# Convolutions and mixings on array tiles of 32 rows and 64 columns instead of 32 rows and 128 columns

## The reference

```python
# x: (128, 128, 2048)  batch, channel, length;   cond: (128, 128);   fside: (128,)
def conv_layer(x, c, weight, c_weight, bias):        # weight (128, 32, 9), 4 groups
    out = lax.conv_general_dilated(x, weight, window_strides=(1,), padding=[(4, 4)],
                                   dimension_numbers=('NCH', 'OIH', 'NCH'), feature_group_count=4)
    return out + jnp.einsum('nd,od->no', c, c_weight)[:, :, None] + bias[None, :, None]

def mixing_layer(x, emb, W0, b0, W1, b1, W2, b2, weight, bias_k):   # weight (8, 128, 128, 1)
    h = gelu(gelu(emb @ W0 + b0) @ W1 + b1)
    att = softmax(h @ W2 + b2)                         # one weighting of 8 experts per sample
    agg_w = jnp.einsum('bk,koi->boi', att, weight[..., 0])
    return jnp.einsum('boi,bih->boh', agg_w, x) + (att @ bias_k)[:, :, None]

x = x + conv_layer(x, cond, w0, c_w0, fside);   x = x + mixing_layer(x, cond, ...)   # layers 0, 1
x = x + conv_layer(x, cond, w2, c_w2, fside);   x = x + mixing_layer(x, cond, ...)   # layers 2, 3
```

## Time and profile before

| | |
|---|---|
| median of 3 runs | 2659.2 us (2658.6 to 2659.79) |
| profiled execution | 2658.37 us, span 2656.6 us |
| PE busy | 2588.4 us (97%), 24,812 matmul records |
| weight loads (PEld) | 1191.4 us (45%) |
| DVE busy | 2148.2 us (81%) |
| ACT busy | 1493.2 us (56%) |
| POOL busy | 36.7 us (1%) |
| DMA | 357.06 MB, mean 134 GB/s |

### The profile page before, as it was taken

The page is one execution under the profiler, slowest core; times in us unless marked ns, Lnnn a source line. Parts: engine busy times, 40 slices in busy tenths (PEclk is TensorE's granted clock), DMA queues, the critical chain, the costliest instruction groups (busy, mean ns, idle before and its releaser), DMA issues.

```text
span 2656.6 us, 57542 instructions
## 1 busy us (share of the span) xinstructions
PE 2588.4 (97%) x24812; PEld 1191.4 (45%) x24812; DVE 2148.2 (81%) x815; ACT 1493.2 (56%) x852; POOL 36.7 (1%) x31
## 2 busy tenths in 40 slices
PE   6689999999999999999999999999999999999998
PEld 4234444444444444444444444444444444444443
DVE  5678888888888888888888888888888888888883
ACT  2345555555555555555555555555555555555554
POOL 5000000000000000000000000000000000000000
PEclk8689999999999999999999999999999999999999
DMA  4543444434434434444344344343443443443433
GB/s 151 205 163 118 155 121 130 146 118 136 140 118 146 130 119 152 123 127 149 118 139 137 118 150 126 120 154 120 132 144 118 139 137 118 148 128 120 153 92 112
DMA packets 185493, 357.06 MB, mean 134 GB/s; under 512 B 12714, under 2 KB 143794, under 8 KB 152634
## 3 DMA queue, kind: packets, MB, share of 16 engines
q1 hardware_dynamic: 184576, 352.37, 42.3%
q10 hardware_dynamic: 898, 4.39, 0.7%
HBM read 205.72 MB, written 150.99 MB: 134 GB/s over the span
## 4 chain that ended last, share of the span: by engine, by line
PE 96%; DMA 2%; DVE 1%; ACT 1%; issue 0%; ACTq 0%; SPq 0%; DVEq 0%
PE psum L350 34%; PE psum L313 33%; PE psum L325 28%; DMA mix_dram<-y 1%; DVE diff L545 0%; DVE y L594 0%; ACT y L464 0%; DMA select_sb<-select 0%; PE psum L274 0%; ACT y L474 0%; PE psum L303 0%; DMA mixw<-mix_dram 0%; ACT x L514 0%; ACT outb L498 0%; DVE att L565 0%
## 5 line engine op out<-in xcount | busy, mean ns | idle before, releaser
L545 DVE TENSOR_TENSOR diff<-xin 128x2052 f32<-128x2052 f32 x256 | 986.7, 3897 | 354.9 <-PE psum L325 354.9
L350 PE MATMUL psum<-y,mixw 32*128 32x512 f32 x8192 | 917.8, 595 | 20.1 <-DMA mixw<-mix_dram 13.7
L313 PE MATMUL psum<-diff,prod_w 32*128 32x512 f32 x8192 | 907.8, 589 | 12.5 <-DVE bias_table L584 7.6
L325 PE MATMUL psum<-diff,prod_w 32*128 32x512 f32 (+1 forms) x8192 | 773.2, 600 | 0.0
L471 ACT COPY shared<-psum 128x2048 f32<-128x2048 f32 x256 | 477.8, 1866 | 381.7 <-PE psum L313 375.4
L350 PEld LDWEIGHTS psum<-y,mixw 32*128 32x128 f32 x8192 | 418.5, 186 | 503.6 <-issue 497.9
L313 PEld LDWEIGHTS psum<-diff,prod_w 32*128 32x128 f32 x8192 | 430.4, 186 | 466.9 <-issue 458.9
L474 ACT COPY y<-psum 128x2048 f32<-128x2048 f32 x256 | 478.1, 1867 | 272.8 <-PE psum L325 272.8
L545 DVE TENSOR_TENSOR diff<-x 128x2055 f32<-128x2055 f32 x256 | 571.1, 2295 | 10.3 <-ACT x L514 10.3
L325 PEld LDWEIGHTS psum<-diff,prod_w 32*128 32x128 f32 (+1 forms) x8192 | 315.8, 158 | 434.2 <-issue 417.4
L514 ACT ACTIVATE x<-psum,bias_now 128x2048 f32<-128x2048 f32 x128 | 252.7, 1974 | 215.8 <-PE psum L350 215.8
(11 more groups left out here) (57 smaller groups left out, 92.4 us busy)
## 6 DMA issues: line engine op xcount, KB each, us to landing
xin<-x SPq DMA_DIRECT2D x128, 1024.0 KB, 6.6
out<-outb SPq DMA_DIRECT2D x128, 1024.0 KB, 4.7
mixw<-mix_dram SPq DMA_DIRECT2D x512, 128.0 KB, 5.2
mix_dram<-y SPq DMA_DIRECT2D x16, 1024.0 KB, 4.4
y<-experts ACTq DMA_DIRECT2D x2, 512.0 KB, 12.4
x<-conv_w ACTq DMA_DIRECT2D x1, 768.0 KB, 9.5
shared<-conv_w ACTq DMA_DIRECT2D x1, 768.0 KB, 10.9
diff<-expert_rows ACTq DMA_DIRECT2D x4, 144.0 KB
```

The lines of the kernel that those rows point to most:

```text
L313: mm = pe.matmul(psum[:, half, g, :], prod_w[v][at, kind, s, :], diff[at, s, :, 0:R], start=first and s == 0, stop=last and s == PH - 1, s ...
L325: return pe.matmul(psum[cols, half, g, :], prod_w[v][at, kind, s, cols], diff[at, s, :, 0:R], start=False, stop=stop, skip_group_check=True)
L350: mm = pe.matmul(psum[:, half, r, :], mixw[m][at, b, g, :], y[m][at, :, g, b, :], start=g == 0, stop=g == GROUPS - 1)
L545: nc.vector.tensor_tensor(into(kind), in0, in1, op).then_inc(diff_ready[v], 1)
```

## The change

Each matmul of 128 columns in `product`, `outer_products` and `mix` becomes two of 64 columns, LOWER (0 to 63) and UPPER (64 to 127), one behind the other for the same group. In the middle part of `outer_products` the sets of 64 columns used to stand as four LOWER, four UPPER; now they alternate group by group, and the wait for the copy of half B moves from behind four LOWER matmuls to behind the first. The raising of `conv_done` for half A stays at the last LOWER matmul of position 1. The other engines' code is unchanged.

```diff
+LOWER, UPPER = slice(0, P // 2), slice(P // 2, P)
...
                         at = slice(CG * g, CG * (g + 1))
-                        mm = pe.matmul(psum[:, half, g, :], prod_w[v][at, kind, s, :], diff[at, s, :, 0:R],
-                                       start=first and s == 0, stop=last and s == PH - 1, skip_group_check=True)
+                        for cols in (LOWER, UPPER):
+                            mm = pe.matmul(psum[cols, half, g, :], prod_w[v][at, kind, s, cols], diff[at, s, :, 0:R],
+                                           start=first and s == 0, stop=last and s == PH - 1, skip_group_check=True)
                 mm.then_inc(conv_done[v], 1)
...
                 pe.wait_ge(shared_ready[v], 2 * n + 1)
                 for s in (3, 2):
                     for g in range(GROUPS):
-                        one_set(ONLY_EVEN, even, A, s, slice(0, P), g, False)
+                        for cols in (LOWER, UPPER):
+                            one_set(ONLY_EVEN, even, A, s, cols, g, False)
                 for s in (0, 1):
                     for g in range(GROUPS):
-                        mm = one_set(ONLY_EVEN, even, A, s, lower, g, s == 1)
-                    if s == 0:
-                        pe.wait_ge(shared_ready[v], 2 * n + 2)
-                    else:
-                        mm.then_inc(conv_done[v], 1)
-                    for g in range(GROUPS):
-                        one_set(ONLY_ODD, odd, B_HALF, s + 2, upper, g, False)
+                        mm = one_set(ONLY_EVEN, even, A, s, LOWER, g, s == 1)
+                        if s == 1 and g == GROUPS - 1:
+                            mm.then_inc(conv_done[v], 1)
+                        if s == 0 and g == 0:
+                            pe.wait_ge(shared_ready[v], 2 * n + 2)
+                        one_set(ONLY_ODD, odd, B_HALF, s + 2, UPPER, g, False)
                 for s in (0, 1):
                     for g in range(GROUPS):
-                        mm = one_set(ONLY_ODD, odd, B_HALF, s, slice(0, P), g, s == 1)
+                        for cols in (LOWER, UPPER):
+                            mm = one_set(ONLY_ODD, odd, B_HALF, s, cols, g, s == 1)
                 mm.then_inc(conv_done[v], 1)
...
                         at = slice(CG * r, CG * (r + 1))
-                        mm = pe.matmul(psum[:, half, r, :], mixw[m][at, b, g, :], y[m][at, :, g, b, :],
-                                       start=g == 0, stop=g == GROUPS - 1)
+                        for cols in (LOWER, UPPER):
+                            mm = pe.matmul(psum[cols, half, r, :], mixw[m][at, b, g, cols], y[m][at, :, g, b, :],
+                                           start=g == 0, stop=g == GROUPS - 1)
                 mm.then_inc(mix_done[m], 1)
```

More of the change, by code:

```diff
@@ L320, in outer_products @@
                 odd = diff_of(v, ONLY_ODD).rearrange("p (s b m) -> p s b m", s=PH, b=PB)
-                lower, upper = slice(0, P // 2), slice(P // 2, P)
                 def one_set(kind, diff, half, s, cols, g, stop):
```

## The result

| | before | after |
|---|---|---|
| median | 2659.4 us | 2708.4 us (2707.15 to 2712.07) |
| ratio | | 1.0187 [1.0174, 1.02] |
| span of the profiled execution | 2656.6 us | 2705.4 us |
| one step of the loop | 39.48 us | 40.24 us |
| PE busy, matmul records | 97%, 24,812 | 96%, 45,292 |

The account below looks back on a forecast made before the run. TensorE was taken to bound the kernel (PE busy 97%). Half A's lateness +0.33 less 0.05 for the bare load gives +0.28 us for each of 128 `outer_products`, 36 us on 2658.4: 2694 us, range 2670 to 2722.

Parts of the forecast that it names:

- products and mixing cost nothing when doubled: Products and mixing: eight tiles run side by side, a round still takes 0.43 us, so twice the matmuls add nothing.
- The rival of feeding and shared banks: Half-width matmuls can't be fed or hinder each other on one bank: much slower, about 3,200 us; chance 0.09.
- the 62 ns for each MATMUL: Skill's rule for the sequencer without hardware decode: about 62 ns a MATMUL, so 45,000 would take 2,790 us.
- Changes of width: Both in `outer_products` go, 0.38 us on the array each time, but the saving does not reach the end.
- The wait holds LOWER: Middle of `outer_products`: LOWER behind the wait for half B's copy runs in step with UPPER, 0.33 to 0.34 us later.
- The first rival: Middle of `outer_products`: LOWER is not held by UPPER's wait, mixing starts 0.21 us earlier, 2631 us; chance 0.10.
- this case's own range: 2682 to 2704 us for the main forecast, from variations in the bare load and TensorE's start behind a semaphore.
- +0.33 for half A's lateness: Per `outer_products`: `conv_done` for half A, and so ScalarE's copy of it, comes 0.33 us later.
- the bare load's 0.05: Mixing's first load, now of 64 columns, is bare for 0.06 instead of 0.11 us, giving back 0.05.
- half of the effect lost: The reason given for the full range's lower end, 2670 us.
- Instruction pages: Loop body grows from 3 to 5.5 pages and may need fetches each step: slower, taken as 2750 us; chance 0.04.

Follow-up runs that it names:

- e1: Changed kernel, but in the middle of the outer products four LOWER matmuls stand ahead of the wait for half B's copy, then four UPPER; 2635.8 us.
- e4: Products and mixing of 64 columns from the changed kernel, `outer_products` from the kernel before; 2685.0 us.
- e7: Kernel before, with the wait for half B's copy moved ahead of the four LOWER matmuls of position 0; 2701.5 us.
- e9: e1 with position 0 as in the changed kernel: one LOWER, the wait, then LOWER and UPPER alternating; 2704.3 us.
- e6: e1 with position 1 as in the changed kernel, LOWER and UPPER alternating; 2709.7 us.
- e8: e1 with one UPPER matmul of position 3 moved ahead of the last LOWER matmul, which raises `conv_done` for half A; 2702.3 us.
- e3: Changed kernel with three LOWER matmuls ahead of the wait and the fourth behind the first UPPER, the same at position 1; 2702.9 us.

## Why the prediction was right, point by point

- *TensorE's row sets the time; products and mixing cost nothing when doubled.* Right: rounds of eight stay 0.43 us apart, PE's busy time is unchanged, and e1 with all matmuls doubled is the fastest kernel here. The rival of feeding and shared banks is gone with e1. Its rounds hold a matmul every 54 ns, so the 62 ns for each MATMUL that the prediction quotes from the Trainium skill beside that rival, with the 2,790 us worked out from it, did not bind either.
- *Changes of width cost 0.38 us on the array, but their saving does not reach the end.* Right. The rule of the Trainium skill ("TensorEngine Tiling (Array Packing)", "Key Properties": a change of tiling mode drains TensorE) agrees with e4 in that a change costs, 0.25 us for the way to 128 columns. The saving shows in the time only in e1, where the end is no longer held.
- *The wait holds LOWER.* Right as to the time and, by e7 and e9, a sufficient cause. The first rival (LOWER let past) fell: 1018.86 and 1019.28 have one load each.
- *The loss comes from that wait alone.* This was incomplete. The signal of half A stands behind three UPPER matmuls of position 3, and by e6 and e8 that alone ties the copy to UPPER. Had the wait let LOWER past, the time would have been the same, as e6 shows with 2709.7 us, and the 2631 us that the prediction gave this rival would not have come; the prediction's statement that the wait decides is true of e7 and not of the changed kernel, which has two causes for one delay.
- *The size.* The measured 2708.4 us is above the 2682 to 2704 that the prediction calls this case's own range, and inside its full range. Forecast +0.28 us for each of 128 outer products, measured +0.38 (0.76 a step). The mis-sized term is +0.33 for half A's lateness: the distance grew by 0.36, and the copy from which it is measured starts a further 0.06 later in the stretch. From the first outer-product load to the second `shared` copy it is 0.31 us now (1017.57 to 1017.88) and was 0.25 (1003.01 to 1003.26). A round of eight is spread over 0.05 to 0.06 us (a row of 0.19 with loads of 0.13), one of four over 0.02 (0.15), and each handover to ScalarE waits for the round's last. 0.36 + 0.06 less the bare load's 0.05 is 0.37. That the spread is all of the 0.06 is argued, not shown. In e8 and e3, with one UPPER matmul ahead of the signal, the distance is 3.90 and the time 6.1 and 5.5 us below the changed kernel's; that fits a spread at the signal, and says nothing of the first copy.
- *Sums.* Two bounds do not follow from the sum: half of the effect lost would be 2676 us, not 2670, and the largest time worked out for the case's own range is 2701, not 2704. Neither decides anything. The 0.23 us between the copy and the mixing's load hold at one of the two handovers of a step; the other has 0.12.
- *Instruction pages.* 29 pages of 16 KB instead of 17 in the whole run, and none between 200 and 2500 us, so none in the loop's steps there. One cost shows at the loop's exit: TensorE rests once, between the last mixing of the loop and the product behind it, where the kernel before does not, and two packets of the instruction queue fall between 2570 and 2590 us. That they cause the rest is likely and not shown. e8 has 2.98 us at this place, so differences of a few microseconds between kernels of 64 columns are not all the loop's.

```profile
2580.18 2.18 issue
```

- *VectorE and DMA.* Neither holds more than 2% of the chain; VectorE's wait for L325 went from 5.72 us a step to 6.12:

```profile
1042.02 7.76 DVE L547 TENSOR_TENSOR diff<-xin 128x2052 f32<-128x2052 f32 x2 [6.12 <-PE psum L325]
```

## What to carry to other kernels

When work for two consumers shares one in-order queue, put all that the first consumer waits for, and its signal, ahead of anything that may wait or end later, even where the two run on separate parts of the engine. A saving on a busy engine is worth only what the next handover lets through; here the same 64-column tiles gave 0.9% or cost 1.9% by the place of one wait and one signal. And check a "sufficient" explanation by removing its cause alone, since a second one may lie under it.

## What the runs showed of the hardware

- Tiles of TensorE run out of step (LOWER 0.33 us ahead of UPPER), but signal in the order of the program. In e6 the signalling matmul was over at 1002.85 by its record, whose end is modelled, and ScalarE started at 1003.48. The Trainium skill has this in "TensorE: Matmul & The Clock Gate", "The cost: per-tile semaphore tail": matmuls complete in the order of the program, so one increment on the last tile is safe. The signals of e6 and e8 agree, and show the other side: an increment in the middle waits for matmuls of other tiles ahead of it, 0.53 us a time and 66 us in all in e8.
- A change of column width on the array costs 0.25 us to 128 columns in e4 and 0.21 in the kernel before, of which 0.11 is the bare weight load; on the way to 64 columns it was 0.17.
- A wait on one weight load held the loads and matmuls behind it, those of free tiles too: in the changed kernel three row tiles get no further load from 1018.43 to 1019.79, and the line moved in e7 costs 0.33 us a time and 42 us in all.
- Eight tiles of 32 by 64, each with its own weight load, hold 0.43 us a round over whole stages (128 records in 6.87 us, L315): a load and a matmul every 54 ns.
